# Attention with one head per 32 rows in fp32, x projection and first dt in a lane of their own, and half the convolution on TensorE

## The reference

```python
# Mamba, layers 0 and 2 (inner width 512, 16 states, dt rank 64, 4 taps)
xm, z = split(h @ W_in, 2)
xm = silu(conv1d(xm, conv_w, causal) + conv_b)
dtr, Bm, Cm = split(xm @ W_xp, [64, 80])
dt = softplus(dtr @ W_dt + b_dt)
hst = hst * exp(dt_t * A) + (dt_t * x_t) * B_t      # over 256 tokens
y = (sum over states of hst * C_t + xm * D) * silu(z)
x = x + gate * (y @ W_out)
# attention, layer 1
att = softmax(q @ k.T + (1 - mask) * -1e6)          # per head, over the keys
y = att @ v                                         # v times mask
x = x + silu(layer_norm(y) * (1 + scale) + shift) @ out_w + out_b
```

## Time and profile before

| | us |
|---|---|
| median of 3 runs (5597.52 to 5597.84) | 5597.71 |
| the profiled execution, its own time | 5590.43 |
| its span in the trace | 5588.7 |

### The profile page before, as it was taken

How to read it: one execution, slowest core, us unless ns; L and a number is a source line. 1 busy time by engine, 2 the same in 40 slices (tenths; PEclk the granted TensorE clock), 3 DMA queues, 4 the chain that set the end, 5 groups by cost and what they waited for, 6 DMA issues and landing times.

```text
span 5588.7 us, 53381 instructions
## 1 busy us (share of the span) xinstructions
PE 4454.7 (80%) x15736; PEld 2303.5 (41%) x15736; DVE 4889.9 (87%) x5146; ACT 3458.5 (62%) x6180; POOL 4081.3 (73%) x2847
## 2 busy tenths in 40 slices
PE   4577888888888888888888888888888888888766
PEld 1233444444444444444444444444444444444323
DVE  3749999999999999999999999999999999999482
ACT  2345666767666666766666676766666676666351
POOL 2718787877878787777888787787878778787271
PEclk8678899999999999999999999999989999999775
DMA  4517676766767666666767676676767667676161
GB/s 146 191 61 231 212 231 210 227 219 211 236 200 232 217 225 220 214 230 205 228 221 228 208 228 226 208 234 209 230 208 225 216 218 232 204 232 213 56 212 49
DMA packets 350126, 1146.07 MB, mean 205 GB/s; under 512 B 38789, under 2 KB 79274, under 8 KB 349834
## 3 DMA queue, kind: packets, MB, share of 16 engines
q1 hardware_dynamic: 305674, 1088.05, 60.3%
q10 hardware_dynamic: 44160, 54.60, 3.0%
HBM read 1123.47 MB, written 19.04 MB: 204 GB/s over the span
## 4 chain that ended last, share of the span: by engine, by line
DVE 48%; PE 21%; issue 10%; ACT 7%; POOL 7%; DMA 6%; SPq 1%; DVEq 0%; ACTq 0%; POOLq 0%
DVE hw L966 23%; DVE ps L952 12%; DMA bs<-bc_scratch 5%; POOL hw L984 4%; DVE u L796 4%; PE ps L1139 3%; PE ps L853 3%; PE ps L1148 2%; DVE mx L1347 2%; PE ps L1131 2%; ACT da L902 1%; PE ps L1200 1%; PE ps L677 1%; DVE stats L594 1%; PE ps L868 1%
## 5 line engine op out<-in xcount | busy, mean ns | idle before, releaser
L984 POOL TENSOR_TENSOR hw<-hw,cs 128x1024 f32<-128x1024 f32 x1024 | 2420.0, 2363 | 865.1 <-DVE hw L966 827.3
L966 DVE TENSOR_TENSOR_SCAN hw<-da,ps 128x1024 f32<-128x1024 f32 x1024 | 2335.0, 2280 | 77.5 <-PE ps L853 11.0
L902 ACT ACTIVATE da<-dt,a_neg 128x510 f32<-128x510 f32 x2048 | 1331.8, 714 | 366.0 <-DVE hw L966 364.1
L952 DVE TENSOR_TENSOR ps<-ps,bs 128x1024 f32<-128x1024 f32 x1024 | 1255.5, 1226 | 119.9 <-DMA bs<-bc_scratch 66.7
L991 POOL TENSOR_TENSOR hw<-hw 128x512 f32<-128x512 f32 x1024 | 1301.3, 1271 | 70.8
L853 PE MATMUL ps<-hw,ident 128*128 128x512 f32 x2048 | 1141.3, 663 | 133.5 <-POOL hw L991 132.0
L672 PE MATMUL ps<-hT,w_in 128*128 128x512 f32 x1024 | 510.4, 633 | 163.7 <-ACT sz L774 84.9
L853 PEld LDWEIGHTS ps<-hw,ident 128*128 128x128 f32 x2048 | 386.4, 207 | 578.0 <-issue 276.6
L1313 ACT ACTIVATE pts<-ps,mcur 128x256 f32<-128x256 f32 x1024 | 400.5, 475 | 238.2 <-PE ps L1236 236.5
L549 ACT ACT_TABLE_LOAD x351 | 450.3, 1283 | 6.4
L1347 DVE TENSOR_REDUCE mx<-ps 128x2 f32<-128x512 f32 x512 | 330.9, 680 | 98.7 <-PE ps L1207 98.3
(11 more groups left out here) (186 smaller groups left out, 6008.6 us busy)
## 6 DMA issues: line engine op xcount, KB each, us to landing
bs<-bc_scratch SPq DMA_DIRECT2D x1024, 512.0 KB, 5.0
cs<-bc_scratch SPq DMA_DIRECT2D x1024, 512.0 KB, 4.1
xhat<-in_x ACTq DMA_DIRECT2D x16, 512.0 KB, 4.6
gate<-gates_scratch ACTq DMA_DIRECT2D x64, 128.0 KB, 5.1
x_b<-in_x ACTq DMA_DIRECT2D x16, 512.0 KB, 6.9
x_scratch<-x_b ACTq DMA_DIRECT2D x16, 512.0 KB, 2.9
x_c<-x_scratch ACTq DMA_DIRECT2D x16, 512.0 KB, 6.2
out<-x_c ACTq DMA_DIRECT2D x32, 256.0 KB, 4.4
```

What stands on the lines that cost most here:

```text
L902: ins = nc.scalar.activation(da[q % (AHEAD + 1)][:, k, :, 1:S], dt_[:, c, :].rearrange("p (b s) -> p b s", b=GB)[:, :, 1:S], ACT.Exp, scal ...
L952: nc.vector.tensor_tensor(z, dxp.unsqueeze(1).broadcast_to([P, 2, T]), bs[s % B_RING][:, :, :], ALU.mult)\
L966: nc.vector.tensor_tensor_scan(tile[:, :, :].rearrange("p n t -> p (n t)"), da[s % (AHEAD + 1)][:, :, :, :].rearrange("p n b s -> p (n b s)"),
L984: nc.gpsimd.tensor_tensor(tile[:, :, :], tile[:, :, :], cs[s % C_RING][:, :, :], ALU.mult)\
```

## The change

Attention: the weights and biases of q and k are laid out on the host so that each head has 32 rows (16 channels and 16 spare ones). Row 16 of each head (`MASK_ROW`) holds 1 in q and the mask row in k; row 17 (`MAX_ROW`) holds 1 in k and, once they are known, the negated maxima in q. So the mask and the maximum come into the product by themselves, and q and k stay in fp32. `stack`, `pick`, `qk`, `nm`, the hi/lo parts and the two halves are gone. VectorE adds the transposed maxima to q (`qa0`, `qa1`, 128x512).

Mamba: the x projection and dt0 move from `front` into pieces `mid0`/`mid1` in lane B, dt1 into `rest`. dt's bias comes in by a row of the matmul; softplus is max(v, 0) + ln(1 + exp(-|v|)), with the absolute value on ScalarE and no cap. Chunks 0 and 2 of the convolution are four matmuls with diagonal matrices `taps`, which are loaded from DRAM (512 KB) for each front; chunks 1 and 3 stay on VectorE. The row biases are an fp32r pair of rows. SyncE issues `cs` of step s-1 behind `bs` of step s. `PLACES` is a new table. GpSimd's instructions in the loop are the same in kind and number.

```diff
+ON_PE = (0, 2)
-HP = PAIRS // 2
+HG = H // 4
+MASK_ROW, MAX_ROW = DH, DH + 1
@@ lanes
-        [("rest0", 0, 0), ("back1", -2, 0), ("lin_a", -2, 0), ("rest1", -1, 1), ("lin_b", -2, 1)]]
+        [("rest0", 0, 0), ("back1", -2, 0), ("lin_a", -2, 0), ("mid1", -1, 0),
+         ("rest1", -1, 1), ("lin_b", -2, 1), ("mid0", 1, 1)]]
@@ front, TensorE
+        def convolve(pc, m):
+            bank = side[pc.bank[f"c{m}"]].rearrange("p (b s) -> p b s", b=GB)
+            xm = u[:, m, :].rearrange("p (b s) -> p b s", b=GB)
+            for s in range(TAPS):
+                ins = nc.tensor.matmul(bank[:, :, s:], taps[:, ON_PE.index(m), (TAPS - 1 - s) * P:(TAPS - s) * P],
+                                       xm[:, :, 0:S - s], start=(s == 0), stop=(s == TAPS - 1),
+                                       skip_group_check=True)
+            ins.then_inc(pc.next(f"c{m}"), 1)
@@ front, VectorE
-            for m in range(IC):
+            for m in (1, 3):
@@ dt
-            nc.vector.tensor_scalar(dt_[:, m, :], side[pc.bank[f"d{m}"]], col(f"m{l}_b_dt", m), EXP_CAP,
-                                    ALU.add, ALU.min).then_inc(pc.next(f"mn{m}"), 1)
+            nc.scalar.activation(dt_[:, m, :], side[pc.bank[f"d{m}"]], ACT.Abs).then_inc(pc.next(f"ab{m}"), 1)
@@ loads of the scan, SyncE
                 slice_in(bs[s % B_RING], s, B_RING, 0, "dbx", b_in)
-                slice_in(cs[s % C_RING], s, C_RING, NS, "mul", c_in)
+                if s:
+                    slice_in(cs[(s - 1) % C_RING], s - 1, C_RING, NS, "mul", c_in)
@@ front, SyncE
+            taps_are_free(sp, l, g)
+            sp.dma_start(taps[:, :, :], taps_dram[l]).then_inc(taps_in[l], 16)
@@ attention, TensorE: transposed scores (scores alike, with q4 and k4 swapped)
-                            nc.tensor.matmul(banks[hh].rearrange("p (h s) -> p h s", h=2),
-                                             pick[:, c0:c0 + 1].broadcast_to([P, P]),
-                                             nm[:, :].unsqueeze(1).broadcast_to([P, 2, S]), start=True, stop=False,
-                                             skip_group_check=True)
...
-                                rr = slice(64 * hh, 64 * hh + 64)
+                            rr = slice(32 * (h % 4), 32 * (h % 4) + 32)
+                            ins = nc.tensor.matmul(banks[hh][:, t * S:(t + 1) * S], k4[rr, h // 4, t * P:(t + 1) * P],
+                                                   q4[rr, h // 4, :], start=True, stop=True)
@@ attention, VectorE
+            for x in range(2):
+                dve.wait_ge(pc.of(f"nm{x}"), pc.upto(n, f"nm{x}"))
+                half = q4[:, 2 * x:2 * x + 2, :].rearrange("p g s -> p (g s)")
+                nc.vector.tensor_tensor(half, half, side[pc.bank[f"nm{x}"]], ALU.add).then_inc(pc.next(f"qa{x}"), 1)
@@ attention, ScalarE
-                            for t in range(RB):
-                                ins = nc.scalar.activation(pt[(2 * p + hh) % 4][:, t, :],
-                                                           side[pc.bank[f"t{p}{hh}"]][:, t * S:(t + 1) * S],
-                                                           ACT.Exp, bias=mcur[:, 1, t:t + 1])
+                        nc.scalar.activation(pts[:, (2 * p + hh) % 4, :], side[pc.bank[f"t{p}{hh}"]], ACT.Exp)\
+                          .then_inc(pc.next(f"x{p}{hh}"), 1)
```

765 lines of the change are left out of this document (410 added, 355 removed), and 11 rows, old and new, of the table PLACES.

## The result

The changed kernel took 5500.3 us (median of 4 runs, 5497.5 to 5503.2) beside 5597.6 us for the kernel before on the same chip: ratio 0.9833, interval 0.9818 to 0.9847. By the medians it is 97 us faster, by the ratio 94 us; 240 us were forecast, and the range was 5250 to 5480 us.

What follows compares the result with a forecast made beforehand. VectorE, 94.3% busy in the middle, was taken as the bound; -253.1 (work), -26 (waits), +45 (TensorE), +15 (GpSimd), -30 (ends) and +9 us (prologue) gave -240.1 us, hence 5358 us; range 5250 to 5480 us.

Steps and rivals of the forecast that it cites:

- Work taken from VectorE: Cap, half the taps, remainders gone, additions new: net 270.0 us less on VectorE, 15/16 counted on the path, -253.1 us.
- The mx wait: VectorE's 36.0 us of waiting for scores before the maxima; bounds 0 and -36, taken as -10 us.
- The bs wait: VectorE's 46.3 us of waiting for bs loads; earlier loads against added taps loads, bounds -46 and +76, taken as 0.
- The nm wait: VectorE's 31.7 us of waiting for ScalarE's copy in the attention; bounds 0 and -31.7, taken as -16 us.
- Crowding at the front: Projections and convolution on TensorE delay the scan's reductions at 32 fronts; bounds 0 and +160, taken as +45 us.
- that rival: TensorE's crowding takes half of the gain: 5478 us, span 5430 to 5580 us, chance 0.22.
- TensorE's sum: TensorE's busy time: 1215.5 us gone, 1077 us new, net 138 us less, from 4455 to about 4317 us.
- The slower rival: The 32-row score tiles don't run side by side, a pair takes 1.81 us; about 5772 us, chance 0.07.
- The sign that I named for it: A pair of scores over 1.5 us and TensorE over 4650 us would mean the 32-row tiles don't overlap.
- ScalarE "hidden, 0 on the path": ScalarE, at 67%, nets -113 us of work including new absolute values for dt; counted as 0 on the path.
- The ends: Attention without a scan at the run's start and end gets shorter: -15 us each, -30 us, bounds 0 and -45.
- The prologue: More weights, diagonals, taps and rows handled before the first load of x: +9 us, bounds +4 and +15.

Runs made afterwards that it cites:

- one-tap kernel: The changed kernel with only one of the four matmuls of each TensorE convolution, the other three taps left out; ratio 0.9931.
- b_sp_order: The kernel before with only the new load order, cs of step s-1 issued behind bs of step s; ratio 0.9890.

## Why the prediction was wrong

**Work taken from VectorE.** The sum held: 249 us gone where 270 net were forecast (the changed groups by line add up to 272.6 us; their records overlap a little). The step that failed is the next one: "30 of the 32 attentions and fronts lie under scans, where VectorE is full, so I count 15/16 of it on the path". VectorE was 94% busy, but 18.4 us of idle time per iteration were taken for a constant. The cap alone, with nothing else changed, was worth 44 of the 95 us of its records, or 27 us with the loads early. The table by stretches gives the rest; these are the same eleven iterations of the kernel before with the new load order only:

```profile
1018.04:4512.97 3494.93, 2934.31 (x10780) 1537.12 (x10780) 3340.99 (x3500) 2373.07 (x4247) 2798.22 (x1937) 0.94 0.68 223
```

That is 317.7 us per iteration with VectorE's work as it was. The load order gave 4.3 us of the 7.1; the 15.7 us of work taken from VectorE, with all that came in for it, gave 2.8. A count in full would have needed the chains beside the scan to have slack of the same size. The row for ScalarE's ln shows one that had none: before, VectorE came up to 0.4 us ahead of its end already, 13 times. The earlier trace rows leaves that row out.

**The mx wait.** I wrote that it falls "if a pair of scores costs TensorE less (below)" and took -10 us; the price below was 1.06 us per pair, and the old pair costs as much. At the upper clock, from its mask passes to the next work, it takes 1.09 us:

```profile
2024.45 0.73 PE L1200 MATMUL ps<-mb,pick 128*128 128x512 f32 x2
2025.11 0.50 PE L1207 MATMUL ps<-qk 64*128 64x256 f32 x4
2025.54 2.84 PE L853 MATMUL ps<-hw,ident 128*128 128x512 f32 x6
```

The condition was never checked against my own number. Measured: 1.13 us at the upper clock, 2.08 us at the lower, +60 us of waits in 732 to 4930 us. With the price of a pair about the same, the dense run of 16 maxima in place of two runs of eight, the lower clock, and a VectorE that has less to do beside them are what is left to explain the +60 us; the runs don't divide it between them.

**The bs wait.** "Nearest to the present row I take 0": wrong by 57 to 62 us in the good direction. The bound at the good end, 46 us, was read from 730 to 4930 us only; the whole span has 66.7 us of these waits. The bad end, taps in the way, was worth about 10 us where 76 were possible.

**The nm wait** went wholly, 31.7 us where 16 were taken. **Crowding at the front**: +45 us was taken for stalls of the ring behind the convolution; L1039's waits for L926 are 11.6 us, far from the 100 us that were to show the crowding. The result lies in that rival's span (5430 to 5580 us), and its number (5478 us) is near, by luck: it got there through a stall that isn't there.

**TensorE's sum** was 234 us short (4317 against 4551.2 us). The groups of scores and convolution on the page:

```profile
L1277 PE MATMUL ps<-k,q 32*128 32x256 f32 x2048 | 354.3, 469 | 112.5 <-DVE mx L1397 112.0
...
L1304 PE MATMUL ps<-q,k 32*128 32x256 f32 x2048 | 301.6, 412 | 21.0 <-ACT pts L1372 21.0
```

That is 655.9 us for 543, 113 us more; the convolution was 229.0 for 255. The other half of the miss lies in the way of adding up. TensorE's groups come to 4878.6 us before and 4853.2 after, by line and shape, 25 us less where 138 were forecast; the total on the page counts overlapping records once and went from 4454.7 to 4551.2. The groups overlapped by 424 us before and by 302 us after. The prediction took whole groups, 1215.5 us, off a total in which part of them was never counted; that is some 122 us. The clock moved too, at the lower level for 649 us in the stretch in place of 526, and single lines of unchanged work with it (L926 1184.0 us, where L853 had 1141.3; L698 534.5 for 510.4 in the earlier trace rows); how much of the 113 us is the clock stays open. The slower rival, tiles one after another, is refuted: 8 passes in 1.13 us are less than 1.81 us. The sign that I named for it, "a pair of scores over 1.5 us", misled: a pair takes 2.08 us at the lower clock with the tiles side by side all the same. The speedup of 3.07 for four tiles that the Trainium skill states (TensorE: Matmul & The Clock Gate, Part 3) could not be seen here, where two run side by side.

**ScalarE "hidden, 0 on the path"** failed at dt: VectorE waits 40.6 us for the end of its chain of three, where it waited 4.8 us.

**The ends.** The prologue was right (first scan step 122.0 for 115.7 us; 9 us estimated). "-15 us for each of the two" was wrong. The attention without a scan takes as long as before: 5108.1 to 5192.6 us here, 85.6 us in the earlier trace rows. And from its end to the last scan it is 57.7 us in place of 40.8. The chain there goes through what I had priced at nothing, the move of the x projection into lane B; the mean granted clock is also lower, 0.81 where it was 0.96. The chain of the end (start, duration, what):

```profile
5230.21 1.94 PE ps L1222 x8
5232.15 0.93 issue
5233.07 3.66 PE ps L722 x8
```

The x projection (L722) waits until the linear attention of lane B has ended; before, it ran beside it (`L660` at 5315.67 us, the out-projection of the linear attention at 5324.53 us). The same order stands in the iterations of the middle, and is the chain that the half clock of the one-tap kernel hit.

**Where the gain comes from** (94 us by the ratio), by steps between kernels that were run: loads -62 us (b_sp_order); attention, dt and the lanes, with the convolution still on VectorE, from 0.9890 to 1.0120, +129 us, though VectorE is busy 121 us less there (4768.6 us); the convolution, from 1.0120 to 0.9833, -161 us. The middle kernel's table wasn't tuned and TensorE is at the lower level for 945 us in it, so the two last numbers may both be too large; how the +129 us divide between the scores' chain and lane B stays open. The change came out faster, which had a chance of 0.90; the range missed it, because the bounds of each cost were set around it and none around the share of saved work that counts.

The best kernel is the changed one with bf16 first scores: 5412 us, ratio 0.9672, 1.6% below the changed kernel. It rounds only the value that is subtracted from all scores of a row; a row whose keys are all masked would need care, which wasn't tried.

## What to carry to other kernels

An engine that is 94% busy is not proof that a microsecond saved on it is one gained: take one saved piece out of the old kernel, alone, and see what share arrives before summing up. When an instruction goes, ask what ran under it; the chain that it covered is the next wait. Add up busy times of one kind only: group times overlap, and don't come off a total that counts overlaps once. Read a wait over the whole span before it bounds a term. Price a chain of producer and consumer by its round trip, and an edit of a queue's order (here two lines of load order) as seriously as one of hundreds of instructions.
